# Channel mix cut into pieces of 12 matmuls and placed between attention heads, on one core

## The chip, the cores and the metric

The kernel is written in Bass, engine by engine, for one NeuronCore of one Trainium2 chip. Each engine (PE is TensorE, ACT ScalarE, DVE VectorE, POOL GpSimd, SP SyncE) runs its own instruction list strictly in the order written; semaphores are all that ties them together. The metric is the device time of one execution in microseconds (us), lower is better.

## The reference, cut to what matters

Input x is [4, 512, 512] (4 sequences of 512 tokens, 512 features). The output is the input plus two branches that both start from its layer norm xn.

```python
xn = layernorm(x)
# branch 1: RWKV style block
x1 = ln(xn); xln = ln(x1)
r = sigmoid(mix(xln, shift(xln)) @ Wr);  vmix = sum_t((xln @ Wv) * decay_t)
x2 = xn + r * (vmix @ Wo + bo)
xc = ln(ln(x2))
vc = square(relu(shift(xc) @ Wck)) @ Wcv      # channel mix, 512 -> 2048 -> 512
branch1 = x2 + sigmoid(xc @ Wcr) * vc
# branch 2: attention (16 heads of 32) and a mixture of 8 experts, top 2
q, k, v = rms(xn) @ Wq, Wk, Wv
h = softmax(causal(q k^T / sqrt(32))) v
xp = xn + h @ Wo
rows = rms(xp); route = top2(rows @ Wr)
branch2 = xp + sum_e weight_e * (silu(rows Wg_e) * (rows Wu_e)) Wd_e
out = x + branch1 + branch2
```

Precision: every large product is done as three fp32r matmuls (`mm3`, lines 49 to 51): each operand is split in a rounded high half and a remainder, and high*high, high*low, low*high are summed in one PSUM bank. The rounding copy is an ACT instruction, the remainder a subtraction on DVE or POOL.

## The kernel before

Four stages follow each other, each a `Block` whose end all engines wait for.

**Time mix** (`time_mix_phase`): norms, v, r, and rc = sigmoid(xc @ Wcr) for the four sequences; writes xn, x2, rc and the halves of xc to DRAM. The change leaves it as it is but for how its semaphores are given back.

**Attention** (`attention_phase`), one sequence b after another in a loop: q, k and v projections (`q`, `k`, `v`, 48 matmuls of 512 columns each), then `heads(b)`, then the output projection `project(b)`, the RMS norm, the transposes (`turn_rows`), the router's logits and the routing on DVE (`routing`, a chain of 15 small dependent operations). q and k are gathered by DMA into "stacks" of 96 rows (high, low, high), so that one matmul gives the exact product. `heads(b)` runs steps s = 0 to 25. Step s computes the scores of head s (`scores`, 4 matmuls plus 4 small bf16 matmuls for the causal mask), of which DVE takes the row maxima (`maxima`). The maxima are transposed in three sets (heads 0-3, 4-9, 10-15), negated, and sent by DMA into row 96 of the stack; from step LAG = 8 on, head s - 8 has its scores computed again transposed with the maximum subtracted (`turned_scores`), ACT takes the exponential in three parts and rounds it (DVE does the rounding for the last eight heads), DVE forms the remainder (`split_probs`), and head s - 10 is multiplied by its values (`head_output`, 12 matmuls). For the first eight steps of every sequence PE has scores alone.

**Channel mix** (`channel_mix_phase`): the 2048 hidden features in 8 chunks of 256; for each chunk the four sequences: `up` (24 matmuls of 512 columns into two banks), relu on ACT, square on DVE, rounding on ACT, remainder on DVE, `down` (24 matmuls into four banks), with `up` of the next sequence issued before `down` of this one. A weight chunk is split once and used for four sequences. `acc`, 128x8192 in SBUF, holds the sum for all tokens. In the same stage POOL places the routed tokens (`Router`): 32 indirect DMAs, lines 688 to 692, that scatter 128 entries each into a table in DRAM.

**Experts** (`experts_phase`): 23 tiles of 256 rows, 4 weight chunks each; writes `acc` to `out` and adds the experts' rows by indirect DMA. POOL waits for the write of `acc` (`base_out`) before its loop.

The order of work is written out by hand in each engine's function; there is no planner.

## Time and profile before

| | |
|---|---|
| time, median of 3 runs | 2159.82 us (2156.29 to 2162.97) |
| the profiled execution | 2163.49 us; its span 2161.7 us; mean granted clock 0.922 |
| PE busy | 1914.1 us, 89% |
| DVE busy | 1202.4 us, 56% |
| ACT busy | 935.3 us, 43% |
| POOL busy | 551.5 us, 26% |

The span is the time from the first to the last instruction. "Granted clock" is the share of 2.4 GHz at which TensorE was let run: 0.50 is its lower level of 1.2 GHz, 1.00 is 2.4 GHz, and a value between is a stretch with both. Matmuls are pipelined and their ends are modelled, so the duration of one matmul (0.39 us for 512 columns) is longer than the distance from one start to the next; the distance is what counts for throughput.

### The profile page before, as it was taken

The numbers are of one execution on the slowest core, as the hardware profiler recorded it, in microseconds if no ns is written. First come the engines' busy times: TensorE is split into PE (matmuls) and PEld (weight loads), VectorE is DVE, ScalarE is ACT, GpSimd is POOL, SyncE is SP. The second block draws the span as 40 slices with busy tenths as digits, with TensorE's granted clock in tenths as the row PEclk, the third lists the DMA queues.
The fourth block names the chain that finished last, engine by engine and source line by source line (L and its number), as shares of the span: only waits on it lengthen the run. The fifth ranks groups of instructions, "written<-read, shape, count | busy, mean of one in ns | idle before, by whom it ended". The sixth has DMA issues, their size and how long they took to land. (4 is left out here: it accounts for less than half of the span.)

```text
span 2161.7 us, 30419 instructions
## 1 busy us (share of the span) xinstructions
PE 1914.1 (89%) x10850; PEld 1634.4 (76%) x10850; DVE 1202.4 (56%) x1794; ACT 935.3 (43%) x1505; POOL 551.5 (26%) x536
## 2 busy tenths in 40 slices
PE   3878667898889889767999997999999999999997
PEld 2666455686677676555888886999999999999986
DVE  6887334835726736543555557555555555555543
ACT  4454333634625525422222222555555555555553
POOL 3233220010010010152000004334444353434443
PEclk9989876996996987877999998999999999999998
DMA  4332352251270260270002015756666565756562
GB/s 175 118 117 97 137 156 60 79 144 33 78 168 8 78 157 1 78 277 9 32 19 79 0 40 208 280 196 202 201 213 216 203 209 201 228 196 206 193 194 49
DMA packets 70275, 288.21 MB, mean 133 GB/s; under 512 B 10375, under 2 KB 10631, under 8 KB 51922
## 3 DMA queue, kind: packets, MB, share of 16 engines
q1 hardware_dynamic: 56514, 262.84, 35.0%
q0 software_dynamic: 11552, 20.55, 5.6%
q10 hardware_dynamic: 2160, 4.19, 0.5%
q8 instruction: 28, 0.46, 0.1%
q14 instruction: 21, 0.17, 0.0%
HBM read 220.47 MB, written 45.84 MB: 123 GB/s over the span
## 5 line engine op out<-in xcount | busy, mean ns | idle before, releaser
L49 PE MATMUL bank<-ex_x_hi,ex_w_hi 128*128 128x256 f32 x1472 | 419.0, 285 | 5.2 <-issue 5.2
L50 PE MATMUL bank<-ex_x_lo,ex_w_hi 128*128 128x256 f32 x1472 | 417.4, 284 | 0.0
L51 PE MATMUL bank<-ex_x_hi,ex_w_lo 128*128 128x256 f32 x1472 | 417.3, 284 | 0.0
L1215 DVE TENSOR_TENSOR ex_w_lo<-ex_stage,ex_w_hi 128x2048 fp32r<-128x2048 f32 x138 | 249.9, 1838 | 147.4 <-ACT ex_w_hi L1160 141.0
L49 PEld LDWEIGHTS bank<-ex_x_hi,ex_w_hi 128*128 128x128 f32 x1472 | 283.1, 192 | 8.2 <-issue 5.6
L50 PEld LDWEIGHTS bank<-ex_x_lo,ex_w_hi 128*128 128x128 f32 x1472 | 283.2, 192 | 2.7
L51 PEld LDWEIGHTS bank<-ex_x_hi,ex_w_lo 128*128 128x128 f32 x1472 | 283.1, 192 | 0.0
L1099 POOL TENSOR_TENSOR ex_a_lo<-ex_a,ex_a_hi 128x256 fp32r<-128x256 f32 x184 | 176.6, 980 | 393.5 <-ACT ex_a_hi L1180 381.5
L1175 ACT ACTIVATE ex_gate<-bank 128x256 f32<-128x256 f32 x184 | 70.7, 384 | 240.7 <-PE bank L51 240.7
L721 ACT ACTIVATE cm_relu<-bank 128x512 f32<-128x512 f32 x64 | 38.3, 599 | 256.8 <-PE bank L51 220.7
L1943 PE MATMUL bank<-at_k,at_q 96*128 96x512 f32 (+3 forms) x256 | 115.4, 546 | 38.0 <-DMA at_k<-at_ones 26.9
L49 PE MATMUL bank<-ex_w_hi,ex_a_hi 128*128 128x512 f32 x368 | 144.6, 393 | 1.7 <-POOL ex_a_lo L1099 1.7
L50 PE MATMUL bank<-ex_w_lo,ex_a_hi 128*128 128x512 f32 x368 | 144.3, 392 | 0.0
L51 PE MATMUL bank<-ex_w_hi,ex_a_lo 128*128 128x512 f32 x368 | 143.2, 389 | 0.0
L1802 DVE TENSOR_REDUCE at_row_max<-bank 128x1 f32<-128x128 f32 (+3 forms) x256 | 107.6, 483 | 44.1 <-PE bank L1945 44.1
L1160 ACT ACTIVATE ex_w_hi<-ex_stage 128x2048 fp32r<-128x2048 f32 x69 | 131.2, 1901 | 1.6 <-DMA ex_stage<-in_w_moe 1.6
L1814 DVE TENSOR_TENSOR at_p_lo<-at_p_full,at_p_hi 128x1280 fp32r<-128x1280 f32 x64 | 95.5, 1493 | 58.8 <-ACT at_p_hi L1673 57.7
L763 DVE SCALAR_TENSOR_TENSOR cm_a<-bank,cm_relu 128x512 f32<-128x512 f32 x64 | 44.2, 690 | 135.4 <-ACT cm_relu L721 122.6
L49 PE MATMUL bank<-cm_x_hi,cm_w_hi 128*128 128x512 f32 x256 | 102.8, 401 | 8.4 <-DVE cm_w_lo L756 8.4
L1667 ACT ACTIVATE at_p_full<-bank 128x512 f32<-128x512 f32 (+1 forms) x192 | 87.0, 526 | 53.0 <-PE bank L1957 51.5
L1236 DVE TENSOR_TENSOR ex_a<-ex_gate,bank 128x256 f32<-128x256 f32 x184 | 72.6, 415 | 65.0 <-ACT ex_gate L1175 61.0
L1943 PEld LDWEIGHTS bank<-at_k,at_q 96*128 96x128 f32 x256 | 75.4, 297 | 41.9 <-DMA at_k<-at_ones 22.7
(268 smaller groups left out, 4484.1 us busy)
## 6 DMA issues: line engine op xcount, KB each, us to landing
ex_stage<-in_w_moe SPq DMA_DIRECT2D x69, 1536.0 KB, 6.3
first_w<-in_w_moe SPq DMA_DIRECT2D x23, 1536.0 KB, 7.5
at_q<-at_q_hi SPq DMA_DIRECT2D x32, 256.0 KB, 5.2
at_k<-at_k_hi SPq DMA_DIRECT2D x32, 256.0 KB, 6.3
cm_stage<-in_w_cm SPq DMA_DIRECT2D x8, 1024.0 KB
tm_x_in<-in_x SPq DMA_DIRECT2D x4, 1024.0 KB, 7.2
scratch_xn<-tm_xn SPq DMA_DIRECT2D x4, 1024.0 KB, 5.3
tm_xn_res<-scratch_xn SPq DMA_DIRECT2D x4, 1024.0 KB, 9.0
```

Of the source, the lines that this page charges most:

```text
L49: pe.matmul(out, lhsT=w_hi, rhs=x_hi, start=first, stop=False)
L50: pe.matmul(out, lhsT=w_hi, rhs=x_lo, start=False, stop=False)
L51: return pe.matmul(out, lhsT=w_lo, rhs=x_hi, start=False, stop=last)
L1099: pool.tensor_tensor(a_lo[:, s % 2, m, :], a[:, m, :], a_hi[:, s % 2, m, :].bitcast(F32), ALU.subtract).then_inc(a_lo_ready, 1)
L1160: act.activation(w_hi[:, c % 2, UP], stage[c][:, UP], ACT.Copy).then_inc(wu_hi_ready, 1)
L1175: act.activation(gate[:, m, :], up_bank[m][:, 0:TILE], ACT.Silu).then_inc(gate_ready, 1)
L1215: return dve.tensor_tensor(dst, src, hi.bitcast(F32), ALU.subtract)
L1236: dve.tensor_tensor(a[:, m, :], gate[:, m, :], up_bank[m][:, TILE:2 * TILE], ALU.mult).then_inc(a_full, 1)
L1667: act.activation(p_full[i % 2][:, at:at + cols], psum[3 + n][:, 0:cols], ACT.Exp, scale=QK_SCALE).then_inc(exp_ready, 1)
L1802: dve.tensor_reduce(row_max[:, j, n:n + 1], psum[bank0 + bank][:, col:col + (j + 1) * P], AX.X, ALU.max).then_inc(max_step, 1)
L1814: dve.tensor_tensor(p_lo[i % 2][:, :], p_full[i % 2][:, :], p_hi[i % 2][:, :].bitcast(F32), ALU.subtract).then_inc(p_lo_ready, 1)
L1943: pe.matmul(out[:, col:col + (j + 1) * P], lhsT=q2[0:STACK, i, j * P:(j + 1) * P], rhs=k2[0:STACK, i, 0:(j + 1) * P], start=True, stop=False)
```

## The change

The attention stage and the channel mix stage are replaced by two others.

**`project_phase`** computes q, k and v of all four sequences in one stage, with PSUM banks 4-7 for q and the transposes and 0-3 for k and v, and writes the halves of q and k and the unsplit v to DRAM.

**`heads_phase`** runs all 64 heads as one pipeline of steps 0 to 70, unrolled on every engine (no loops). LAG is 5; the maxima are turned in sets of 4 heads. The q and k stacks are rings of 8 slots filled by six DMAs of 64 KB per head, v comes per pair of heads. Channel mix and output projection are "pieces" of 12 matmuls of 512 columns: `up` (128 hidden features of one sequence), `down` (128 tokens, four hidden chunks) and `proj`; 64 + 64 + 16 = 144 pieces, in the order up, up, up, up, down, down, down, down, with the four `proj` of a sequence let in when its heads are done. Steps 0 to 4 and 64 to 70 have two pieces each, the 59 steps between share 94, and pieces 118 to 143 follow after the last step. All `up` pieces share one PSUM bank and all sums share another. Weights come in slices of 128x512 through a ring of six, and are loaded and split again for every sequence: 144 slices. There is no `acc` for all tokens: `out` is filled with x by DMA, and x2, the projection's rows and the gated channel mix are added to it by accumulating DMAs from POOL, each of which waits for the one before. Routing of a sequence is done after its projection; the scatter of the router's table (32 indirect DMAs) stands in POOL's list at piece 129.

```diff
+    LAG = 5
+    SLOTS = 8
+    SET = 4
+    RAW = 6
+    DEEP = 4
+    CHUNKS = I_CM // (DEEP * P)
+    STEPS = N + LAG + 2
+    FIRST_PROJ = HEADS + LAG + 2
+    def pieces_before(s):
+        early = 2 * min(s, LAG)
+        middle = 94 * min(max(s - LAG, 0), N - LAG) // (N - LAG)
+        late = 2 * max(s - N, 0)
+        return early + middle + late
+        S_BANK, T_BANK = psum[0:2], psum[2:4]
+        o_bank, up_bank, sum_bank, misc_bank = psum[4:8]
...
+        @block.sync
+            load_slot(0)
+            for w in range(RAW):
+                load_slice(w)
+            load_slot(1)
+            load_mix(0)
+            for g in range(2, SLOTS):
+                load_slot(g)
+            sp.dma_start(vecs[:, :, :], d["vecs"]).then_inc(const_in, 16)
+            sp.dma_start(wr[:, :, :], d["w_r"]).then_inc(const_in, 16)
...
+        @block.gpsimd
+            def add_rows(k, b, j, src):
+                pool.wait_ge(added, 16 * adds_before[k])
+                at = b * S + j * P
+                pool.dma_start(d["out"][at:at + P, :], src[:, j, :], accum_op=ALU.add, max_dma_last_dim=4 * H).then_inc(added, 16)
...
+                if k == count_at + 2:
+                    pool.wait_ge(table_filled, 16)
+                    pool.wait_ge(route.step, route.SLOTS)
...
+        @block.scalar
+            def begin(k):
+                for w in fresh[k]:
+                    weight(w)
+                kind, b, c, m = order[k]
+                if kind == "up":
+                    n = ups_before[k]
+                    act.wait_ge(up_done, n + 1)
+                    act.activation(relu[:, m, :], up_bank[:, :], ACT.Relu).then_inc(relu_ready, 1)
+            for s in range(STEPS):
+                i = s - LAG
+                ks = pieces(s)
+                for k in late:
+                    finish(k)
+                for k in ks[:1]:
+                    begin(k)
+                if 0 <= i < N:
+                    exps(i, 0)
+                    exps(i, 1)
+                for k in ks[:1]:
+                    finish(k)
+                if 1 <= i <= N and i % 2 == 0:
+                    inverse_sums(i // 2 - 1)
+                if 0 <= i < N:
+                    exps(i, 2)
+                    high_p(i)
...
+                for k in ks[1:]:
+                    begin(k)
+                if s % SET == 0 and SET <= s <= N:
+                    max_row(s // SET - 1)
+                late = ks[1:]
...
+        @block.vector
+            def begin(k):
+                kind, b, c, m = order[k]
+                if kind == "up":
+                    n = ups_before[k]
+                    dve.wait_ge(relu_ready, n + 1)
+                    dve.scalar_tensor_tensor(a[:, m, :], up_bank[:, :], 0.0, relu[:, m, :],
+                                             ALU.max, ALU.mult).then_inc(a_full, 1)
...
+                for w in fresh[k]:
+                    weight(w)
+            def finish(k):
+                if kind == "up":
+                    dve.wait_ge(a_hi_ready, n + 1)
+                    dve.tensor_tensor(a_lo[:, m, :], a[:, m, :], a_hi[:, m, :].bitcast(F32),
+                                      ALU.subtract).then_inc(a_lo_ready, 1)
+            for s in range(STEPS):
+                if s < N:
+                    maxima(s, 0)
+                    maxima(s, 1)
+                for k in late:
+                    finish(k)
+                if 1 <= i <= N:
+                    low_p(i - 1)
+                if s % 2 == 0 and 0 <= s // 2 - 4 < N // 2:
+                    output(s // 2 - 4)
+                for k in ks[:1]:
+                    begin(k)
+                if s < N:
+                    maxima(s, 2)
...
+                for k in ks[:1]:
+                    finish(k)
...
+                for k in ks[1:]:
+                    begin(k)
+                late = ks[1:]
...
+        @block.tensor
+            def up(k, b, c, m):
+                pe.wait_ge(w_lo_ready, slice_at["up", b, c, m] + 1)
+                n = ups_before[k]
+                if n:
+                    pe.wait_ge(a_full, n)
+            def total(k, left_hi, left_lo, j):
+                n = sums_before[k]
+                if n:
+                    pe.wait_ge(sum_taken, n)
+            def down(k, b, c, j):
+                pe.wait_ge(w_lo_ready, slice_at["down", b, c, DEEP - 1] + 1)
+                pe.wait_ge(a_lo_ready, ups_before[k])
+            pe.wait_ge(x_zero, 3)
+            pe.wait_ge(consts_ready, CONSTS)
+            pe.wait_ge(const_in, 32)
+            for s in range(STEPS):
+                if s < N:
+                    scores(s, 0)
+                    scores(s, 1)
+                for k in ks[:1]:
+                    piece(k)
+                if s < N:
+                    scores(s, 2)
+                if 0 <= i < N:
+                    turned(i, 0)
+                    turned(i, 1)
+                if 1 <= i <= N:
+                    head_output(i - 1)
+                if 0 <= i < N:
+                    turned(i, 2)
+                for k in ks[1:]:
+                    piece(k)
+                if s % SET == 0 and SET <= s <= N:
+                    turn_maxima(s // SET - 1, misc_free[0])
+            for k in range(pieces_before(STEPS), PIECES):
+                piece(k)
```

```diff
 def experts_phase(...)
-            for b in range(B):
-                sp.dma_start(d["out"][b * S:(b + 1) * S, :].rearrange(tokens, p=P),
-                             acc[:, b * TT:(b + 1) * TT, :]).then_inc(base_out, 16)
...
-            pool.wait_ge(base_out, 16 * B)
 def build(nc, d):
         time_mix_phase(nc, psum, ident[:, :], d)
-        attention_phase(nc, psum, ident[:, :], ident_bf[:, :], causal[:, :], causal_t[:, :], d)
-        channel_mix_phase(nc, psum, d, routing, acc, stage, first_tile)
-        experts_phase(nc, psum, ident[:, :], routing, first_tile, acc, d)
+        project_phase(nc, psum, ident[:, :], d)
+        heads_phase(nc, psum, ident[:, :], ident_bf[:, :], causal[:, :], causal_t[:, :], routing, first_tile, route, d)
+        experts_phase(nc, psum, ident[:, :], routing, first_tile, d)
```

A piece that is the second of its step is called late below: ACT and DVE finish it only in the next step.

## Rows read from the trace of the kernel before

**Rows 1.** Busy time by stage: us, PE, PEld, DVE, ACT, POOL busy (instructions), granted clock, DMA share, GB/s
```profile
0.00:268.60 268.60, 184.70 (x744) 142.54 (x744) 186.54 (x396) 116.64 (x169) 89.23 (x82) 0.91 0.35 129
268.60:932.90 664.30, 559.47 (x2864) 440.76 (x2864) 351.77 (x587) 288.43 (x532) 55.33 (x24) 0.83 0.32 88
932.90:1333.30 400.40, 363.69 (x1538) 292.62 (x1538) 216.09 (x320) 90.27 (x136) 63.66 (x60) 0.94 0.19 69
1333.30:2161.70 828.40, 806.21 (x5704) 758.49 (x5704) 447.97 (x491) 439.98 (x668) 343.29 (x370) 0.99 0.61 202
```

**Rows 2.** Same view, two stretches of the first sequence's heads
```profile
345.00:355.00 10.00, 10.00 (x41) 6.93 (x40) 7.59 (x21) 0.59 (x1) 0.95 (x1) 0.50 0.00 1
...
375.00:385.00 10.00, 9.51 (x65) 7.65 (x65) 7.95 (x15) 7.58 (x13) 0.00 (x0) 1.00 0.00 0
```

**Rows 3.** Timeline of PE, one step between heads: start, us, instruction
```profile
377.05 0.50 PE L1943 MATMUL bank<-at_k,at_q 96*128 96x512 f32 x1 [0.49 <-DVE at_row_max L1802]
...
378.17 0.48 PE L1955 MATMUL bank<-at_q,at_k 97*128 97x512 f32 x1
...
379.28 0.47 PE L1979 MATMUL bank<-at_p_hi,at_v_hi 128*128 128x512 f32 x1
...
381.15 0.45 PE L1943 MATMUL bank<-at_k,at_q 96*128 96x512 f32 x1
```

**Rows 4.** Busy time in two stretches of the channel mix
```profile
971.00:995.00 24.00, 9.71 (x20) 4.75 (x19) 1.38 (x2) 0.60 (x1) 15.94 (x17) 0.61 0.02 2
...
1060.00:1120.00 60.00, 60.00 (x263) 49.07 (x262) 34.42 (x48) 16.11 (x23) 0.00 (x0) 1.00 0.09 35
```

**Rows 5.** Timeline of all engines inside the first of them
```profile
985.48 0.59 PE L50 MATMUL bank<-cm_w_lo,cm_a_hi 128*128 128x512 f32 x1 [1.52 <-issue]
985.79 0.96 POOL L690 DMA_INDIRECT scratch_table<-rt_pair,rt_places  x1 [0.30 <-issue]
...
989.00 0.59 PE L51 MATMUL bank<-cm_w_hi,cm_a_lo 128*128 128x512 f32 x1 [2.94 <-issue]
```

**Rows 6.** Groups of instructions: busy us, mean ns | idle before, releaser
```profile
L1814 DVE TENSOR_TENSOR at_p_lo<-at_p_full,at_p_hi 128x1280 fp32r<-128x1280 f32 x64 | 95.5, 1493 | 58.8 <-ACT at_p_hi L1673 57.7
L775 DVE TENSOR_TENSOR acc<-bank,acc 128x512 f32<-128x512 f32 x128 | 85.4, 686 | 29.8 <-PE bank L51 24.7 <-issue 2.9 <-remote 2.2
L763 DVE SCALAR_TENSOR_TENSOR cm_a<-bank,cm_relu 128x512 f32<-128x512 f32 x64 | 44.2, 690 | 135.4 <-ACT cm_relu L721 122.6 <-issue 12.6
L1673 ACT ACTIVATE at_p_hi<-at_p_full 128x1280 fp32r<-128x1280 f32 x32 | 40.7, 1272 | 17.6 <-PE bank L1981 17.4
L721 ACT ACTIVATE cm_relu<-bank 128x512 f32<-128x512 f32 x64 | 38.3, 599 | 256.8 <-PE bank L51 220.7 <-issue 20.9 <-remote 15.2
```

**Rows 7.** Timeline, the step's maxima and exponentials, four and three together
```profile
379.37 1.68 DVE L1802 TENSOR_REDUCE at_row_max<-bank 128x1 f32<-128x128 f32 x4
379.50 1.36 ACT L1667 ACTIVATE at_p_full<-bank 128x512 f32<-128x512 f32 x3 [0.29 <-PE bank L1957]
```

**Rows 8.** Timeline, start of the attention stage
```profile
268.67 0.38 SPq L1513 DMA_DIRECT2D at_xn<-scratch_xn  x1
...
270.59 1.04 SPq L1563 DMA_DIRECT2D at_w_stage<-in_w_at  x2
...
288.12 0.76 PE L49 MATMUL bank<-at_x_hi,at_w_hi 128*128 128x512 f32 x1 [3.18 <-DVE at_x_lo L1774]
```

**Rows 9.** Timeline of DVE, first and last of 12 routing operations
```profile
927.41 0.19 DVE L1858 TENSOR_REDUCE at_top<-at_logits 128x4 f32<-128x32 f32 x1
...
929.87 0.16 DVE L1871 TENSOR_TENSOR at_gap<-at_top 128x4 f32<-128x4 f32 x1
```

**Rows 10.** DMA issues: KB each, us from issue to landing
```profile
scratch_xn<-tm_xn SPq DMA_DIRECT2D x4, 1024.0 KB, 5.3
scratch_rc<-tm_mix ACTq DMA_DIRECT2D x4, 256.0 KB, 2.0
```

**Rows 11.** Timeline, PE in the experts' first tile
```profile
1363.61 0.50 PE L49 MATMUL bank<-ex_w_hi,ex_a_hi 128*128 128x512 f32 x1 [0.83 <-POOL ex_a_lo L1099]
```

More of the change, by code:

```diff
@@ new lines, in high_x, with high @@
+            def high_x(b):
+                for c in range(HC):
+                    act.wait_ge(x_turned, b * HC + c + 1)
+                    act.activation(x_hi[:, b % 2, c, :], psum[HC + c][:, :], ACT.Copy,
+                                   scale=vecs[:, V_W1, c:c + 1]).then_inc(x_hi_ready, 1)
+            def high(dst, bank, done, ready, out, b):
+                for m in range(HC):
+                    act.wait_ge(done, b * HC + m + 1)
+                    if b and m == 0:
+                        act.wait_ge(out, b * 16)
+                    act.activation(dst[:, m, :], psum[bank + m][:, :], ACT.Copy).then_inc(ready, 1)
@@ L1817, in output @@
-            def output(b, n):
-                c, half, _, _ = stack(2 * n)
-                own = slice(half * PAIR, (half + 1) * PAIR)
-                dve.wait_ge(rec_ready, b * HEADS + 2 * n + 2)
-                dve.tensor_tensor(o[own, c, :], psum[6 + n % 2][0:PAIR, :], sums_rec[0:PAIR, :],
-                                  ALU.mult).then_inc(o_ready, 1)
-            def heads(b, more):
-                for s in range(HEADS + LAG + 3):
-                    if s < HEADS:
-                        maxima(b, s, 3 * (s % 2) if s < LAG else 0)
-                    if s == LAG - 2 and more:
-                        mean(0, b + 1)
-                    if s >= LAG + 4 and (s - LAG) % 2 == 0:
-                        output(b, (s - LAG - 4) // 2)
-                    if LAG <= s < HEADS + LAG:
-                        split_probs(b, s - LAG)
-                    if s == WO_AT:
-                        low_wo(b)
@@ L1908, in _, with low_x, low @@
-            low_o(B - 1)
-            residual(B - 1)
-            routing(B - 1)
+            def low_x(b):
+                for c in range(HC):
+                    dve.wait_ge(x_hi_ready, b * HC + c + 1)
+                    dve.scalar_tensor_tensor(x_lo[:, b % 2, c, :], psum[HC + c][:, :], vecs[:, V_W1, c:c + 1],
+                                             x_hi[:, b % 2, c, :].bitcast(F32), ALU.mult,
+                                             ALU.subtract).then_inc(x_lo_ready, 1)
+            def low(dst, hi, bank, hi_ready, ready, out, b):
+                for m in range(HC):
+                    dve.wait_ge(hi_ready, b * HC + m + 1)
+                    if b and m == 0:
+                        dve.wait_ge(out, b * 16)
+                    dve.tensor_tensor(dst[:, m, :], psum[bank + m][:, :], hi[:, m, :].bitcast(F32),
+                                      ALU.subtract).then_inc(ready, 1)
@@ L1912, in _, with turn @@
+            mean(0)
+            low_w(0)
+            dve.wait_ge(vecs_in, 16)
+            low_x(0)
+            low_w(1)
+            low_w(2)
+            for b in range(B):
+                low(q_lo, q_hi, HC, q_hi_ready, q_lo_ready, q_lo_out, b)
+                if b + 1 < B:
+                    mean(b + 1)
+                low(k_lo, k_hi, 0, k_hi_ready, k_lo_ready, k_lo_out, b)
+                if b + 1 < B:
+                    low_x(b + 1)
         @block.tensor
         def _(pe):
-            def turn(src, bank, done):
+            def turn(b):
+                pe.wait_ge(norm_ready, b * TT + TT)
@@ L1922, in by_feature @@
+            def by_feature(n, b, bank, done):
                 for m in range(HC):
+                    if n == 1 and b:
+                        pe.wait_ge(v_ready, (b - 1) * TT + m + 1)
                     for k in range(HC):
@@ L1949, in turned_scores @@
-            def turned_scores(n):
-                i = stack(n)[3]
-                for kt in range(TT):
-                    bank, col = PT_AT[kt]
-                    out = psum[3 + bank]
-                    pe.matmul(out[:, col:col + (TT - kt) * P], lhsT=k2[0:STACK + 1, i, kt * P:(kt + 1) * P],
-                              rhs=q2[0:STACK + 1, i, kt * P:S], start=True, stop=False)
-                    last = pe.matmul(out[:, col:col + P], lhsT=ident_bf, rhs=causal_t, start=False, stop=True)
-                last.then_inc(turned_scores_done, 1)
```

1626 lines of the change are left out of this document (837 added, 789 removed).

## The prediction

> **What bounds the kernel now.** I read the busy time by stage first [rows 1]. Time mix (268.6 us) and experts (828.4 us) are hardly touched. The change lives in the attention stage, 664.3 us, and the channel mix, 400.4 us: together 1064.7 us. In the experts PE is busy 97% at clock 0.99. In attention the clock is 0.83 and PE idles 105 us, although no other engine is above 53%. The stretches show why: while a sequence has only scores to compute, the clock is 0.50, and 41 matmuls fill 10 us; once heads flow, it is 1.00 with 65 matmuls in 10 us [rows 2]. In the channel mix nearly all loss is in one place: from 971 to 995 PE gets 20 matmuls in 24 us, at its lower clock in most of it, with "issue" as what it waited for, while POOL issues one indirect DMA after another [rows 4, 5].
>
> So PE sets the end of both stages, and what can be won is its idle time and slow clock. Its necessary work at full clock:
> - A head: scores 377.05 to 378.17 (1.12 us), transposed scores to 379.28 (1.11), values to 381.15 (1.87): 4.10 us [rows 3]. 64 heads: 262.
> - A piece: 263 matmuls in 60 us are 0.228 us each [rows 4]. I take 0.23, so 12 matmuls are 2.76 us; 144 pieces: 397.
> - q, k, v: 4 x 144 x 0.23 = 132.
>
> **Part 1, the projection stage.** The first projection matmul stood 19.5 us after the first load of its stage [rows 8]; the order up to there is the same: 19.5. Then 132 of matmuls, 7.5 for the cold start and three sets of transposes, and the drain: evacuation 0.6, a 1 MB store 5.3 [rows 10], issue and barriers 5: 11. q and k use different banks and the norm of the next sequence (about 9 us of ACT, DVE and POOL) lies beside k's 11 us, so I cost these at nothing. If that cover fails, 2 us per sequence. Sum 170: from 268.6 + 2 (semaphores given back) to 441.
>
> **Part 2, the head stage before its first matmul.** PE waits for `const_in`, and `vecs` and `wr` stand behind 6 + 6 + 6 + 2 + 36 = 56 DMAs in SP's list. SP issues a DMA in 0.52 us (two in 1.04) [rows 8]: 58 x 0.52 = 30, landing 4. PE starts at 441 + 34 = 475. Bounds: 25 if small DMAs issue faster, 45 if the 6.6 MB ahead of them hold the queue.
>
> **Part 3, PE's work in it.** 262 + 397, rows turned and logits 18, maxima 6, 5 for the cold start: 688.
>
> **Part 4, PE's new waits.** The order is fixed on every engine, so I walked the steps. A step with one piece is 4.1 + 2.8 = 6.9 us of PE, one with two 9.6. Per step DVE has maxima 1.68 [rows 7], remainder 1.49, and for `up` 0.69 + 0.69 [rows 6], half an output 0.34, a weight slice 0.6 (an estimate from the 0.69 of other operations on 512 columns) and 0.5 of values: about 6.0. ACT has 1.36 [rows 7] + 1.27 + 0.60 for relu [rows 6], and by the same row 0.6 for each of rounding and weight slice, 1.1 for sums and values: 5.5. Both fit, with DVE the closer. What does not fit is latency:
> - Step 0 to 4, nothing between the pieces but scores: 8.
> - `up` after a late `up` (12 times by the placement): the bank is free after relu 0.60 and product 0.69 plus 0.1, but PE has only two parts of scores, 0.75, to fill: 0.65 each, and DVE's remainder of the probabilities then comes 0.5 later than wanted: 14.
> - `down` after a late `up` (7 times): it needs the last remainder. DVE does product to 1.35, weight to 2.0, the next head's first three maxima to 3.4, then the remainder to 4.1; PE wants it at 0.75: 3.35 each, 23. This is the dearest wait in the pipeline.
> - Maxima row: ACT copies it after everything else of a step; copy 0.6, DMA 2.0 [rows 10]. In the 6 single steps of the 16 it lands 1.3 late: 8.
> - Output bank shared by all pairs: in some 12 odd single steps the inverse of the sums is 0.5 late: 6.
> - Routing of three sequences: 12 chained operations from 927.41 to 930.03 [rows 9], 2.6 on DVE, of which some 2 show: 6.
> - Steps 64 to 70: 6.
> - The 26 pieces after the last step: nothing is between them. Four `up` cost 3 x 1.35 and the change to `down` 2.65, four `down` 3 x 0.7 = 8.8 per eight pieces: 26, and 10 for the last routing, placing and norm.
> - The 32 scatters: 32 x 1.26 = 40 us, each 0.96 and 0.30 before it [rows 5]. Before, PE got 20 matmuls in 24 us of such a train, worth 4.6 at full rate: 19.4 lost [rows 4]. The new code is as new to the engines at that place: 20. Bounds 0 and 40.
> - After the last piece: one accumulating DMA, table, first tile's rows: 12. No row shows an accumulating direct DMA; a plain 1 MB store lands in 5.3, a 256 KB one in 2.0 [rows 10]; I take 6 for the last, bounds 2 and 20.
> Sum 139. Below it could be 60 if an engine ahead covers half of these, above 220 if DVE's wait on ACT lengthens each step.
>
> One rule of the Trainium skill speaks against the burst's term. "Runtime: NRT & Kernel Launch", section "Instruction fetch mechanics", says that a long straight program is streamed by each engine's sequencer itself and the crossing of a block is mostly hidden, while a taken branch can cost a fetch stall. That speaks for unrolled code. The trace agrees in that no such "issue" stretch stands in the long straight lists of the heads, and disagrees in the 24 us of rows 4 and 5. By the rule the 20 would be 0 and the time 2107.
>
> **Part 5, experts.** No write of `acc`. POOL had waited for it, but PE lost only 0.83 us [rows 11]: -1, so 827.
>
> **Sum.** 475 + 688 + 139 = 1302, where the experts began at 1333.3 [rows 1]. 1302 + 827 = 2129 span, and 1.8 around it (2163.49 less 2161.7): 2131, which is 32.5 less than the profiled run. That run was 3.7 above the median, so I say 2127 against 2159.82, 1.5% faster. What the old stages wasted, eight steps of scores at half clock in each sequence, does go; start-up, unfilled latencies and the tail take most of it back: 170 + 34 + 688 + 139 + 2 = 1033 against 1064.7.
>
> **Rivals.**
> - Engine coupling (slower). DVE is at 6.0 of 6.9 us in a single step with `up`; if each wait adds to the next, DVE becomes the bound of the step. Its place is DVE's list between `low_p` and the last maxima. 1 us per step over 64 steps gives 2191; it decides for slower from 0.5 us per step. For it: DVE's remainder already waited 57.7 us on ACT in 32 heads [rows 6]. Against: with a piece, PE's own step is 2.8 us longer than it was then.
> - Supply of the unrolled lists (slower). If the 36 accumulating DMAs from POOL starve the engines as the scatters did, at 1.5 us each: 54 more, 2181. Against: they are single, not a train.
> - Waits mostly hidden. Pieces give every latency 2.76 us of cover; late `up` to `down` and the tail stay, half the rest goes, and the burst with it: 139 becomes 75, 2063.
> - The burst costs nothing, with the rest as forecast: 2107.
> - The clock does not stay up: the change doesn't do what it says. The tail has PE at 2.76 of 4.1 us. A stretch with PE busy 9.5 of 10 us was at 1.00 [rows 2], one with 9.7 of 24 at 0.61 [rows 4]; the tail lies between. If the last 26 pieces ran at half clock, 70 more: 2197.
>
> **How the numbers follow.** A measurement of this kernel can tell 0.3% from no change, 6.5 us: 2153.3 to 2166.3. Forecast 0.34 (its own range 2095 to 2155), burst free 0.12, waits hidden 0.22, coupling 0.18, supply 0.08, clock 0.06. Faster: 0.34 + 0.12 + 0.22 less 0.05 at the forecast's upper end: 0.63. Same: that 0.05 and 0.04 from the lower ends of the slow cases: 0.09. Slower: 0.32 less 0.04: 0.28. The range reaches into both sides: 2045 to 2195.
>
> **What would show it.** Project stage near 170 us with PE without gaps over 2 us. First matmul of the head stage 34 us after its first load. Clock 1.00 from there to the tail. Waits of `down` for the remainder `a_lo`, some 3.4 us each, 7 times, and of `up` for `a`. A stretch of "issue" waits on all engines while POOL scatters, some 20 us. Steps of 6.9 and 9.6 us; if they are 8 and 11, coupling is right and I am wrong. If PE's idle sum in the head stage after its start is under 80, the third rival is right.

## The result, and the profile after

The changed kernel takes 2183.52 us (median of 8 runs, 2169.88 to 2185.85) against 2159.01 (8 runs, 2155.81 to 2165.19): ratio 1.0099, 95% interval [1.0075, 1.0123]. It is 1.0% slower; 2127 had been forecast. The profiled execution took 2173.18 us with a span of 2171.3.

Busy time by stage: time mix, projections, the head stage before its first matmul, the rest of it, experts (columns as in [rows 1]):

```profile
0.00:269.40 269.40, 184.52 (x744) 142.57 (x744) 186.55 (x396) 116.68 (x169) 89.26 (x82) 0.91 0.35 129
269.40:440.20 170.80, 145.79 (x640) 118.29 (x640) 43.26 (x58) 65.57 (x117) 8.39 (x11) 0.91 0.47 170
440.20:464.60 24.40, 0.00 (x0) 0.00 (x0) 2.83 (x6) 2.62 (x5) 0.00 (x0) 0.50 0.89 255
464.60:1344.00 879.40, 736.61 (x3778) 575.36 (x3778) 492.20 (x917) 430.74 (x800) 82.85 (x97) 0.95 0.43 115
1344.00:2171.30 827.30, 805.53 (x5704) 758.04 (x5704) 447.93 (x491) 440.01 (x668) 344.32 (x370) 0.99 0.61 197
```

Projections (forecast 170) and experts (827) came out as worked out. The start was 10 us better than forecast: a small DMA takes SP 0.42 us, where [rows 8] had 0.52:

```profile
448.40 0.42 SPq L1002 DMA_DIRECT2D hd_q<-scratch_q_hi  x1
```

All of the error is in the fourth row: 879 for 827. The same view, cut at steps 0 to 4, 5 to 63, 64 to 70, the 26 pieces after the last step (the tail), and what follows the last matmul:

```profile
464.60:515.70 51.10, 41.90 (x170) 31.53 (x170) 23.78 (x46) 13.02 (x24) 4.47 (x4) 0.87 0.99 267
515.70:1117.90 602.20, 547.45 (x2963) 431.60 (x2962) 376.19 (x699) 347.12 (x642) 29.71 (x32) 0.97 0.42 113
1117.90:1190.30 72.40, 60.26 (x285) 46.75 (x284) 39.88 (x57) 36.68 (x65) 3.48 (x4) 0.95 0.45 128
1190.30:1326.80 136.50, 87.00 (x362) 65.48 (x362) 50.96 (x114) 33.92 (x71) 41.31 (x53) 0.91 0.25 62
1326.80:1344.60 17.80, 0.00 (x0) 0.01 (x1) 1.39 (x2) 0.01 (x1) 3.91 (x5) 0.63 0.47 101
```

By the forecast's own terms these were 46, 578, 60, 132 and 12. The clock of the second row is 0.97, although no other engine is near its limit: something makes PE fall back to 1.2 GHz now and then. The timeline shows where. PE and DVE around one change from `up` to `down` (start, us, instruction, idle before it and what ended it):

```profile
625.15 0.23 PE L1506 MATMUL bank<-causal_t,ident_bf 128*128 128x128 bf16 x1
627.53 0.49 DVE L1395 TENSOR_TENSOR hd_v_lo<-hd_v_raw,hd_v_hi 128x128 fp32r<-128x128 f32 x2 [2.93 <-ACT hd_v_hi L1234]
627.94 0.69 DVE L1348 TENSOR_TENSOR hd_a_lo<-hd_a,hd_a_hi 128x512 fp32r<-128x512 f32 x1
628.73 0.76 PE L48 MATMUL bank<-hd_down_hi,hd_a_hi 128*128 128x512 f32 x1 [3.35 <-issue]
629.29 0.63 PE L49 MATMUL bank<-hd_down_lo,hd_a_hi 128*128 128x512 f32 x1
...
631.42 0.57 PE L48 MATMUL bank<-hd_down_hi,hd_a_hi 128*128 128x512 f32 x1
631.83 0.39 PE L49 MATMUL bank<-hd_down_lo,hd_a_hi 128*128 128x512 f32 x1
```

PE pauses 3.35 us, and the next six matmuls start 0.43 us apart; from the eighth on it is 0.23. So this pause cost 3.35 and 1.4 more (3.10 us for seven matmuls that take 1.7 elsewhere). The release is put down to "issue", but the remainder `a_lo` ended at 628.63, just before. It stood behind `low_v`, which waited 2.93 us for ACT, ahead of it in DVE's list.

The length of a pause alone does not say whether the half clock follows. The same `down`, the first of step 64, stood 3.16 us in this execution and in one of the unaltered kernel in a later session (`e_same_2` below):

```profile
1121.12 0.77 PE L48 MATMUL bank<-hd_down_hi,hd_a_hi 128*128 128x512 f32 x1 [3.16 <-DVE hd_down_lo L1303]
1121.69 0.63 PE L49 MATMUL bank<-hd_down_lo,hd_a_hi 128*128 128x512 f32 x1
```
```profile
1121.11 0.47 PE L48 MATMUL bank<-hd_down_hi,hd_a_hi 128*128 128x512 f32 x1 [3.16 <-DVE hd_down_lo L1303]
1121.42 0.39 PE L49 MATMUL bank<-hd_down_lo,hd_a_hi 128*128 128x512 f32 x1
```

The first took 5.26 us for its twelve matmuls, the second 2.87. In the first execution a pause of 1.97 us (at 752.0) was followed by a piece of 5.26, one of 2.51 (at 940.7) by one of 2.87.

A `down` piece without any pause, and the `up` behind it:

```profile
1139.44 0.48 PE L48 MATMUL bank<-hd_down_hi,hd_a_hi 128*128 128x512 f32 x1
1142.32 0.40 PE L48 MATMUL bank<-hd_x_hi,hd_up_hi 128*128 128x512 f32 x1
```

2.88 us for twelve matmuls, where I had taken 2.76 from the average of [rows 4]: the first after scores takes 0.32, the others 0.233.

PE's waits in the head stage: us in total, times, longest:

```profile
PE bank L48 <- DVE hd_a L1310: 46.4, 23, 15.6
PE bank L1490 <- DMA hd_wr<-in_w_r: 34.0, 1, 34.0
PE bank L48 <- issue: 25.0, 11, 3.4
PE bank L48 <- DVE hd_down_lo L1303: 18.4, 7, 3.2
```

The scatters, as in [rows 5], inside the tail:

```profile
1282.00 0.63 ACT L1159 ACTIVATE hd_down_hi<-hd_raw 128x512 fp32r<-128x512 f32 x1 [19.27 <-remote]
...
1288.69 0.96 POOL L1132 DMA_INDIRECT scratch_table<-rt_pair,rt_places  x1 [0.30 <-issue]
1293.18 0.60 ACT L1168 ACTIVATE hd_relu<-bank 128x512 f32<-128x512 f32 x1 [10.55 <-remote]
...
1294.65 0.77 PE L48 MATMUL bank<-hd_x_hi,hd_up_hi 128*128 128x512 f32 x1 [15.65 <-DVE hd_a L1310]
```

PE had written the bank that the relu reads by 1279.0, and ACT was free from 1282.6; it stood 10.55 us, until 3.5 us after the last scatter had been made, and PE waited 15.65 for it. (Of the 19.27 before, all but 6 was a wait for PE's sums.) At the end POOL's accumulating DMAs wait for each other:

```profile
1330.96 0.86 POOL L1105 DMA_DIRECT2D out<-hd_acc  x1 [7.88 <-DMA out<-hd_acc]
1335.35 0.86 POOL L1105 DMA_DIRECT2D out<-hd_acc  x1 [3.54 <-DMA out<-hd_acc]
```

### The profile page after: what moved, and what is told of

Its sections match the earlier page's. It is cut to its first block and busy times, and to the rows that moved or that the text cites. A ratio compares the mean times of both kernels' runs of the same rounds, so it can differ in the third digit from the quotient of the medians.

```text
span 2171.3 us, 30573 instructions
## 1 busy us (share of the span) xinstructions
PE 1872.4 (86%) x10866; PEld 1594.3 (73%) x10866; DVE 1172.8 (54%) x1866; ACT 1055.6 (49%) x1758; POOL 524.8 (24%) x560
## 5 line engine op out<-in xcount | busy, mean ns | idle before, releaser
L1214 ACT ACTIVATE hd_p_full<-bank 128x512 f32<-128x512 f32 (+1 forms) x192 | 94.4, 528 | 140.7 <-PE bank L1506 139.9
L48 PE MATMUL bank<-hd_down_hi,hd_a_hi 128*128 128x512 f32 x256 | 112.1, 438 | 47.7 <-issue 22.8
L48 PE MATMUL bank<-hd_x_hi,hd_up_hi 128*128 128x512 f32 x256 | 108.1, 422 | 46.4 <-DVE hd_a L1310 46.4
L1366 DVE TENSOR_REDUCE hd_row_max<-bank 128x1 f32<-128x512 f32 (+3 forms) x256 | 113.0, 483 | 36.4 <-PE bank L1492 36.3
L1105 POOL DMA_DIRECT2D out<-hd_acc x16 | 14.0, 875 | 437.4 <-DVE hd_acc L1327 401.2
L1490 PE MATMUL bank<-hd_k,hd_q 96*128 96x512 f32 (+3 forms) x256 | 81.4, 375 | 37.0 <-DMA hd_wr<-in_w_r 34.0
L50 PE MATMUL bank<-hd_down_hi,hd_a_lo 128*128 128x512 f32 x256 | 106.6, 416 | 0.0
L49 PE MATMUL bank<-hd_down_lo,hd_a_hi 128*128 128x512 f32 x256 | 106.1, 415 | 0.0
```

Of the source, the lines that this page charges most:

```text
L48: pe.matmul(out, lhsT=w_hi, rhs=x_hi, start=first, stop=False)
L49: pe.matmul(out, lhsT=w_hi, rhs=x_lo, start=False, stop=False)
L50: return pe.matmul(out, lhsT=w_lo, rhs=x_hi, start=False, stop=last)
L1214: act.activation(p_full[:, i % 2, at:at + T_COLS[part]], T_BANK[n % 2][:, 0:T_COLS[part]], ACT.Exp, scale=QK_SCALE).then_inc(exp_ready, 1)
L1366: i = dve.tensor_reduce(row_max[:, j, g % (2 * SET):g % (2 * SET) + 1], S_BANK[n % 2][:, col:col + (j + 1) * P], AX.X, ALU.max)
L1490: pe.matmul(bank[:, col:col + (j + 1) * P], lhsT=q2[0:STACK, g % SLOTS, j * P:(j + 1) * P], rhs=k2[0:STACK, g % SLOTS, 0:(j + 1) * P], sta ...
```

## The experiments

Ratios are to the kernel before in the same session. In the stretches, "tail" is the 26 last pieces, "end" the time from their last matmul to the first instruction of the experts' stage; they are 136.5 and 17.8 us in the profile above.

**The changed kernel again** (two sessions, no edit).

> The changed kernel once more, as the base of the other runs. Its eight runs fell into two groups, 2170 to 2173 us at a mean granted clock of 0.950 and 2181 to 2186 at 0.944 to 0.947. Expected 2183 again, ratio 1.010. If a profile of the longer kind is caught, the 11 us should stand in one stage with a lower granted clock there; if they are spread over all stages the two groups are not a matter of one stretch.

> The changed kernel unaltered, on the same chip as its neighbours here, because the chips differ (the kernel before took 2158 us in one session and 2141 in another). Expected ratio 1.010; and if the difference of the chips stands in the scatter train, the tail of 26 pieces differs with it.

Ratios 1.0099 [1.0064, 1.0134] and 1.0112 [1.0094, 1.0130]. Both profiles are of the longer kind. Steps 5 to 63 took 605.4 and 602.6 us (602.2 above), the tail 146.4 and 150.9:

```profile
1189.30:1340.20 150.90, 97.30 (x363) 72.98 (x362) 50.93 (x114) 34.10 (x71) 40.92 (x53) 0.84 0.23 56
```

So the longer kind is longer mostly in the tail, at clock 0.84 for 0.91. The profile first shown is of the shorter kind, 10 us under the median. The difference is for the larger part half clock and not waiting: by the count used in the table further down, the tail loses 4.4 us to the half clock in the first profile, 11.8 and 14.9 in these two, while PE's pauses in it sum to 49.5, 52.0 and 53.6. Before the tail's first piece PE stood 2.6 us in all three; the piece took 3.05, 4.43 and 5.48.

**DVE: the late remainder ahead of the maxima.**

```diff
+                for k in late:
+                    finish(k)
                 if s < N:
                     maxima(s, 0)
                     maxima(s, 1)
-                for k in late:
-                    finish(k)
```

> Only the order in VectorE's list changes: the remainder of a late `up` piece now stands ahead of the next head's first two groups of maxima. Theory (the wait of `down` for that remainder costs twice, as a gap and as a lower clock after it): the seven gaps of 3.2 to 3.4 us between a late `up` and a `down` shrink to about 1.3 (relu 0.60, product 0.69, rounding 0.63, remainder 0.69, less 0.9 of PE's scores), 14 us; the pieces after them, which took 4.1 to 5.3 us instead of 2.87, are back at 2.87, another 10 us. Together -24: about 2159, ratio 0.999. Rival 1 (the clock falls for another reason, the mean load): 14 us only, the long pieces stay: ratio 1.0035. Rival 2 (coupling of the engines): the maxima come 0.7 us later, the next scores wait for their bank, and nothing is won: ratio 1.010.

1.0092 [1.0061, 1.0123]: 24 us expected, 3 found, which the intervals can't tell from none. The trace (second and third line: start of a `down`):

```profile
627.00 0.49 DVE L1395 TENSOR_TENSOR hd_v_lo<-hd_v_raw,hd_v_hi 128x128 fp32r<-128x128 f32 x2 [2.92 <-ACT hd_v_hi L1234]
861.71 0.77 PE L48 MATMUL bank<-hd_down_hi,hd_a_hi 128*128 128x512 f32 x1 [2.33 <-DVE hd_down_lo L1303]
862.27 0.63 PE L49 MATMUL bank<-hd_down_lo,hd_a_hi 128*128 128x512 f32 x1
```

I had the cause of these gaps half right. Where `up` was a late piece and maxima stood in the way, 3.4 us became 2.3 (the rest is relu, product, a weight slice and the remainder, one after another), and the half clock after it stayed: 4.4 us for the piece. One gap fell from 2.31 to 1.17 and was followed by a piece of 2.87 (4.42 before); another fell to 1.27, and its piece still took 4.67. In two of the cases (here 3.35, unchanged) `up` was the step's first piece, and its remainder stood behind `low_v`, which the forecast had not looked at. After step 63 there are no maxima and 3.15 stayed.

**PE: a `down` waits for each chunk when it comes to it.**

```diff
-                pe.wait_ge(w_lo_ready, slice_at["down", b, c, DEEP - 1] + 1)
-                pe.wait_ge(a_lo_ready, ups_before[k])
-                total(k, lambda q: a_hi[:, q, :], lambda q: a_lo[:, q, :], j)
+                def ready(q):      # called before the three matmuls of chunk q, j == 0 only
+                    pe.wait_ge(w_lo_ready, slice_at["down", b, c, q] + 1)
+                    pe.wait_ge(a_lo_ready, ups_before[k] - DEEP + 1 + q)
+                total(k, lambda q: a_hi[:, q, :], lambda q: a_lo[:, q, :], j, ready)
...
```

The first `proj` of a sequence waits for its weight slices in the same way.

> The first of four `down` pieces waits for each activation chunk and weight slice when it comes to it, not for all four before its first matmul, so nine of its twelve matmuls can run ahead of the last remainder. Theory: each `up` to `down` gap of 3.35 in the heads and 2.85 after them falls by 2.07 us (nine matmuls of 0.23), 11 times, and the half-clock pieces behind them go: 23 + 12 = 35 us: ratio 0.994. The wait then shows inside the piece, 1.3 us. Rival (the clock answers to any pause, not to its length): the long pieces stay and 20 us are won: ratio 1.001. Rival (the remainder is only the last of several things late): under 10 us.

0.9894 [0.9858, 0.9930]: 44 us off the changed kernel, and faster than the one before. Steps 5 to 63:

```profile
511.90:1088.20 576.30, 535.37 (x2963) 421.50 (x2964) 375.75 (x699) 347.35 (x642) 29.65 (x32) 1.00 0.45 120
```

26 us less, for the same instructions: PE idle 40.9 us for 54.8 (the length of the row less PE's busy time), time lost to half clock in the pieces 1.6 for 11.6, clock 1.00 for 0.97.

**PE: useless work in the pause.**

```diff
+                if j == 0:
+                    ...
+                    for _ in range(9):
+                        pe.matmul(sum_bank[:, :], lhsT=a_hi[:, 0, 0:P], rhs=down_hi[:, 0, :], start=True, stop=True)
                 pe.wait_ge(w_lo_ready, slice_at["down", b, c, DEEP - 1] + 1)
                 pe.wait_ge(a_lo_ready, ups_before[k])
```

> Nothing is moved: before the first `down` of each chunk PE runs nine extra matmuls of 512 columns (2.07 us) on operands that are ready, into the bank that the piece then overwrites, and only then waits for the last remainder as before. So a pause of 3.35 us becomes 2.07 of useless work and 1.3 of pause. Theory (the lower clock in the piece after such a gap comes from PE's pause): the long pieces of 4.1 to 5.3 us go back to 2.87, 10 to 15 us less in the head stage although no wait is shorter, offset by up to 2 us at the few places where there was no wait to fill: ratio 1.010 less 0.005 = 1.005. Rival (the clock has another cause than the pause, or dummy work adds its own time): long pieces stay, ratio 1.010 or above.

1.0052 [1.0030, 1.0074], with 1.0112 [1.0094, 1.0130] for the unaltered kernel in the same session: as the theory had it. The place shown above, now:

```profile
623.16 2.34 PE L1567 MATMUL bank<-hd_down_hi,hd_a_hi 128*128 128x512 f32 x9
626.70 0.47 PE L48 MATMUL bank<-hd_down_hi,hd_a_hi 128*128 128x512 f32 x1 [1.20 <-issue]
627.00 0.39 PE L49 MATMUL bank<-hd_down_lo,hd_a_hi 128*128 128x512 f32 x1
```

No operand was ready sooner, 144 matmuls came on top, and the kernel is 12 us (0.6%) faster: after 1.20 us of pause the matmuls take 0.39, after 3.35 they took 0.63. This shows that PE's standing idle brings the half clock. Whether the one long pause or the idle time of the stretch as a whole decides, it doesn't separate.

**The scatters: left out, and spread.** `e_no_scatter` makes only the first of the 32 and its experts work on the table's fill, so only its head stage is to be read. `e_paced` and `e_paced_2` are one kernel in two sessions:

```diff
                 if k == count_at + 2:
                     ...
-                    ...                                  # all 32
+                if k >= count_at + 2:
+                    first = k - count_at - 2
+                    if kind == "up":
+                        pool.wait_ge(a_full, ups_before[k])
+                    else:
+                        pool.wait_ge(sum_taken, sums_before[k])
+                    for i in range(32 * first // (PIECES - count_at - 3), ...):
```

> 31 of the 32 scatters that write the routing table are left out, so the experts work on the fill of the table; only the head stage is to be read. Theory (the train of indirect DMAs keeps the other engines' instruction lists from being supplied): the gap of 15.65 us at 1294 falls to the 1.5 us of every other `up` after `up`, and the two pieces at half clock (4.65 and 5.47 us) become 3.0, in all 14 + 4 = 18 us in the stretch from the first tail piece to the last, 136.5 to about 119. Rival (the engines' own lists wait for something else at that place, such as a code page that has to be fetched anyway): the 15 us gap stays, at most 3 us less.

> The 32 scatters are all there, but spread over the last 15 pieces, two or three in each, each group held until PE has come to its piece. Leaving them out had taken 17 us (against the shorter kind of run) to 27 us (against the longer) from the tail. Theory A (an uninterrupted train starves the others' instruction lists, and any pause lets them through): the tail is near 120 us as without them, ratio 1.001. Theory B (each scatter costs the others a fixed share, wherever it stands): no change, the gaps are cut smaller but their sum stays 17 or more: ratio 1.009.

> The spread scatters once more, now beside the unaltered kernel on one chip. Before, its tail took 119.9 us, as long as with the scatters left out, but its ratio to the kernel before was 1.0119. Theory A (a pause between groups lets the other engines' lists through): tail 120, and 10 to 17 us less in all than the unaltered kernel beside it. Theory B (the train costs the same however it is cut): within 4 us of it.

Left out: 1.0012 [0.9994, 1.0029], with 1.0099 for the unaltered kernel in the same session. Spread: 1.0119 [1.0102, 1.0136] in a session where the kernel before took 2141.59, and 1.0019 [1.0004, 1.0033] in the session of the unaltered kernel's 1.0112. The tail with them left out:

```profile
1193.40:1313.30 119.90, 84.60 (x362) 63.88 (x362) 50.96 (x114) 33.93 (x71) 10.62 (x22) 0.97 0.28 70
```

And with them spread (second session; 119.9 us in the first):

```profile
1197.30:1322.80 125.50, 90.17 (x362) 67.93 (x362) 51.00 (x114) 33.98 (x71) 39.55 (x50) 0.92 0.27 61
```

By the medians of one session each, leaving the train out took 18 us off (2163.01 for 2181.37) and spreading it 22 (2161.40 for 2183.33). The two tails of the shorter kind, 136.5 and 119.9, differ by 17. Against the tails of the longer kind it would be 27 to 31, but part of that is the half clock behind pauses that have nothing to do with scatters: the spread tail just shown has 5.5 us more of it than the one without scatters, at pauses of 35.4 and 35.3 us. In groups of two or three the train costs nearly nothing (theory A): the pauses fell from 53.6 in the unaltered kernel of that session.

The other session, of `e_paced`, `e_ends`, `e_ring` and `e_all`, is no test of that, for there an unbroken train held nobody up either. `e_ends` below leaves the train as it was: 32 scatters, 1.26 us apart, from 1231.7 to 1272.8. Its tail, and ACT inside the train:

```profile
1170.70:1296.50 125.80, 90.45 (x362) 68.05 (x362) 50.94 (x115) 33.93 (x71) 42.83 (x55) 0.92 0.28 68
```
```profile
1260.16 0.63 ACT L1163 ACTIVATE hd_down_hi<-hd_raw 128x512 fp32r<-128x512 f32 x1 [13.58 <-PE bank L50]
1262.89 0.60 ACT L1172 ACTIVATE hd_relu<-bank 128x512 f32<-128x512 f32 x1 [2.10 <-PE bank L50]
```

Both waits end with PE's sums and none with "remote", and PE's pauses in the tail sum to 35.3 us, as without scatters. `e_ring`, with its train unbroken too, has none either. So the spread kernel had nothing to win in that session, and its 1.0119 fits that. The kernel before was 17 us faster there, about what its own train cost in [rows 4]; no profile of it was taken in that session, so that this is the reason is not shown. What changes between sessions stays open; the session of `e_same` and this one have the same chip number on record.

> The kernel before once more, for its profile on this chip: where the scatters stood between 971 and 995 us it had 20 matmuls in 24 us. If the chips differ in what the train costs, this stretch is shorter on a chip where the whole kernel takes 2141 and the same where it takes 2158.

It took 2155.74 us, beside a median of 2157.55: not the fast session that was wanted, but its stretch of scatters differs from that of [rows 4]. This run:

```profile
970.00:995.00 25.00, 15.46 (x51) 10.10 (x50) 4.47 (x7) 2.03 (x4) 16.24 (x17) 0.74 0.02 1
```

The profile before:

```profile
970.00:995.00 25.00, 10.58 (x24) 5.31 (x22) 1.38 (x2) 0.60 (x1) 16.63 (x18) 0.63 0.02 2
```

27 matmuls more, and a span 7.7 us shorter. What a train costs changes from one execution to the next in the old kernel too.

**The ends.** SP's order: first head, constants, four weight slices, input, then the rest. In POOL the gathers of the experts' first tile stand before the last accumulating DMA, and (with DVE's wait for them altered to fit):

```diff
             def add_rows(k, b, j, src):
-                pool.wait_ge(added, 16 * adds_before[k])
+                if j == 0:
+                    pool.wait_ge(added, 16 * adds_before[k])
```

> Only the two ends of the head stage change. Start: the two constant loads stand second in SyncE's list and the first weight slices and the sequence's input before the other seven heads' loads, where the changed kernel has 54 DMAs ahead of the constants and PE begins 24.4 us after the stage before. Theory: PE begins its scores some 20 us sooner, waits once for the 2 MB of input, and is 12 us ahead after step 4. End: the four accumulating DMAs of a sequence no longer wait for each other and the first tile's gathers stand before the last one, where 17.85 us lie between the last matmul and the experts: 8 to 10 us. Together -20: ratio 1.001. Rival (the loads' bytes, not their order, set the start; the last adds are limited by their own landing): -5, ratio 1.008.

1.0009 [0.9992, 1.0025]. PE's first matmul, and its first of a piece:

```profile
440.21 0.76 PE L1494 MATMUL bank<-hd_k,hd_q 96*128 96x512 f32 x1 [10.27 <-DMA hd_wr<-in_w_r]
...
450.22 0.76 PE L48 MATMUL bank<-hd_x_hi,hd_up_hi 128*128 128x512 f32 x1 [8.21 <-DMA hd_x_lo<-scratch_xc_lo]
```

24 us sooner at the first, 17 at step 5 (498.8 for 515.7), the rest going to a wait for 2 MB of input; end 11.7 for 17.8. As expected, a little more at the start and less at the end. The medians agree: 2141.63 is 25 us under the spread kernel of the same session.

**Three banks in turn in the tail.**

```diff
+        def bank_of(k):
+            if k < TAIL:
+                return up_bank if order[k][0] == "up" else sum_bank
+            return psum[5 + k % 3]
...
```

> In the 26 pieces after the last head, the pieces take three PSUM banks in turn (the banks of `up`, of the sums, and the one that turned maxima), and a piece waits for the piece three before it to be read. Theory (each of these pieces waits for one bank to be read): the gaps of 1.50 after an `up` (8 of them) and of 0.88 after a sum (12) go, 12 + 11 = 23 us; of the 6.6 us gap at the routing chain 5 goes too; the 2.85 before a `down` and the scatter train stay: -25, ratio 0.998. Rival (VectorE and ScalarE are the bound once PE runs ahead): the gaps only change their place, under 8 us won.

1.0019 [1.0004, 1.0033]. The tail is 34 us shorter than in the profile above:

```profile
1187.10:1289.70 102.60, 84.46 (x363) 67.94 (x362) 50.90 (x114) 33.56 (x71) 41.68 (x52) 0.90 0.31 72
```

But 17 us of that are what the train cost in that profile, and where `e_ring` was run it cost nothing. Against the spread kernel's tail there, 119.9, the three banks are worth 17 where 25 had been expected. The end grew from 17.8 to 22.0: POOL's scatters ended at 1285, so its four accumulating DMAs came after them.

**Everything together, and three ends to it.** `e_all`: all the above, and a first `up`'s remainder ahead of `low_v`. `e_best`: scatters one train again, the last accumulating DMA ahead of the gathers, the first expert's weights asked for before the table. `e_all_2`: that with the scatters spread.

> All edits together: waits per chunk before the first `down` (measured alone -43), the remainder of a late `up` first in VectorE's step and that of a first `up` ahead of the values' remainder, the ends, the three banks, the spread scatters. If they act in different places their gains add: 43 + 3 + 20 + 25 + 15, less some 8 that the waits per chunk and the banks both count: 2183 - 98 = 2085, ratio 0.966. If what is left is bound by VectorE's and ScalarE's lists (coupling), the sum is missed by more than a third: over 2115.

> As the kernel with all edits, with three changes at its end. There the tail of 26 pieces took 91 us where 136 to 151 stood before, but 23 us lay between the last matmul and the experts, because POOL's 32 scatters (47 us with what stands between them) now end 6 us after the last piece, the gathers stood ahead of the last accumulating DMA, and that one was issued 11 us before the experts began. Now the scatters are one train again, the last accumulating DMA stands ahead of the gathers, and the first expert's weights are asked for before the table. Theory (POOL's chain of scatters, table, gathers is what the end waits for): 23 becomes 15 to 17, ratio 0.9758 less 0.003 = 0.973, if the train does not starve the other engines. Rival (the train without pauses starves them again, as it did in the changed kernel): the tail is 10 to 20 us longer, ratio 0.98.

> The last kernel with its scatters spread over the pieces again, nothing else. Theory (a train without pauses keeps ScalarE's list from being supplied: it waited 14.3 us until the train had ended, and the tail took 117.6 us against 91.1): the tail is back near 91 to 95 us, and the end stays near the 17.5 us it now has or falls to 15: 26 - 23 + 6 = about 25 us less than the last kernel where the train hit it, ratio 0.9763 - 0.011 = 0.965. Rival (the two kernels differ by chance, the train hits one execution and not another): within 8 us of it, ratio 0.973 or above, with a `remote` wait of 8 us or more on ScalarE or VectorE in the tail.

Ratios 0.9758 [0.9742, 0.9774], 0.9763 [0.9747, 0.9779], 0.9678 [0.9662, 0.9695]. The tail of `e_all`:

```profile
1139.90:1231.00 91.10, 83.16 (x363) 65.47 (x362) 50.84 (x114) 33.57 (x71) 39.55 (x50) 0.94 0.36 82
```

That of `e_best`, and ACT in it:

```profile
1141.80:1259.40 117.60, 91.50 (x363) 70.29 (x362) 50.88 (x114) 33.35 (x71) 42.32 (x54) 0.85 0.28 66
```
```profile
1240.16 0.60 ACT L1177 ACTIVATE hd_relu<-bank 128x512 f32<-128x512 f32 x1 [14.33 <-remote]
```

PE itself, inside one `up` piece, whose twelve matmuls have no wait between them:

```profile
1231.02 0.39 PE L49 MATMUL bank<-hd_x_lo,hd_up_hi 128*128 128x512 f32 x1 [2.20 <-issue]
...
1233.12 0.59 PE L50 MATMUL bank<-hd_x_hi,hd_up_lo 128*128 128x512 f32 x1 [1.71 <-issue]
```

And that of `e_all_2`:

```profile
1141.80:1242.40 100.60, 89.63 (x362) 69.80 (x362) 51.08 (x114) 33.22 (x71) 39.33 (x51) 0.88 0.32 76
```

In time the gains add: `e_all` took 2088.90 where 2085 was expected (not in the ratio, 0.966, as the kernel before was faster there too; the 15 us counted for the spread scatters were to be had without spreading in that session). Its end was 22.9 us, because PE now finishes before POOL's 32 scatters. `e_best` shortened the end to 17.5, but its train held ACT for 14.33 us and lost 26 in the tail: the rival came true. With the scatters spread the tail is at 100.6, with 4.3 us of such a wait left and an end of 18.6, and the kernel at 2090.52 against 2160.95, 3.2% faster than the kernel before. It falls between the theory's 91 to 95 and the rival. `e_best` and `e_all_2` come from two sessions with one profile each, in both of which the kernel before took its usual time (2158.82 and 2160.95).

## Why the prediction was wrong

Counted over the 880 us from the first matmul to the experts (a piece lasts from its first matmul to the next instruction, less the pause; time over 2.87 in pieces beyond 3.2 is put down to the half clock):

| term | forecast | measured |
|---|---|---|
| 144 pieces at full clock | 397 | 413 (2.87 each) |
| half clock (forecast: the cold start) | 5 | 23 |
| heads, rows, logits, maxima | 286 | 299 |
| pauses, end included | 139 | 141 |
| drain before a pause | 0 | 4 |

- **New waits: right in sum, by luck in part.** 139 forecast, 141 found. The waits of `up` for the product, of `down` for the remainder (seven at 3.2 to 3.4 us, forecast 3.35), of the sums' bank in the tail and the tail's sum of 56 (measured 49) are where they were said to be. But two of the 3.35 had another cause (`low_v`), and no step of mine held DVE's wait for ACT inside its own list.
- **The failed step: a pause was priced by its length alone.** I counted the late `up` to `down` at 7 x 3.35 and wrote "Clock 1.00 from there to the tail". Behind most of these PE ran at 1.2 GHz for some seven matmuls and more: 12 us in steps 5 to 63, 23 in all in this execution and 30 and 33 in the two of the longer kind, against 5. The useless matmuls show that PE's idling is the cause, and the waits per chunk that it need not be: half clock in steps 5 to 63 fell to 1.6. What decides whether a given pause is followed by it is open: the same 3.16 us was and was not, and pauses of 1.3 us were in two places. The rows for it were there: [rows 5] has matmuls of 0.59 us, at a clock of 0.61 in [rows 4], behind pauses of 1.52 and 2.94, and I read them as the scatters' doing alone.
- **A piece mis-sized.** 2.87, not 2.76: 16 us. 263 matmuls in 60 us [rows 4] is 0.228, a long run without a change of kind; I even rounded up, but left out the first matmul after scores, 0.32.
- **Heads and rows** are 13 over: the heads' matmuls took 271 for 262, in part at half clock, rows and logits 21 for 18, the maxima 6 as forecast.
- **Burst.** Forecast 20, found 17 by the profiles and 18 to 22 by the medians: right where the train costs anything, and nothing in one session of the six, which was the rival at 2107. The 10 us between that profile and the median are for the larger part half clock, not the burst. The Trainium skill ("Runtime: NRT & Kernel Launch", "Instruction fetch mechanics") says that the next instructions are streamed while the engine works and a crossing is mostly hidden. With single DMAs about, and under the train in `e_ends` and `e_ring`, the runs agree; under the train in the other sessions they do not (ACT stood 10.55 us). That PE waits for no semaphore there is shown where it stopped for 2.20 and 1.71 us inside a piece; that instructions are what is missing, for PE and behind ACT's "remote", is my reading.
- **Start and end.** 24 for 34, 18 for 12: the chain of four accumulating DMAs, each waiting for the one before, not one.
- **Rivals.** Engine coupling would have had steps of 8 and 11. Counted from one head's first scores to the next, waits included, the median step took 7.5 us with one piece and 11.0 with two, so by that sign alone it would nearly stand. But it works by adding waits, and the waits came out as forecast (141 for 139); what is over in a step is the piece's size and the half clock. The time it gave (2191) is near, its mechanism is not. (By my own band of 0.3% it decides for slower from 0.6 us per step, not 0.5.) Supply by 54 more and waits mostly hidden (139 becoming 75) are ruled out by the same 141. The clock rival named the tail alone; the loss was at the longer pauses, in the heads as well. In the first profile the tail's gaps of 0.9 to 1.5 left pieces at 3.02; in `e_same_2` one of 1.32 was followed by a piece of 4.40.

The profiled run adds up: 42 us over the forecast's span = 53 in the table, 10 less at the start, 1 in rounding. The median adds 10 for the longer kind and 4 because the profile before stood above its median.

So the expected gain of 32 us was to be had only if the fixed order left no such pause. The old stages lost their time in eight steps of scores at half clock; the new one loses it in many small places, some of them paid twice. Of the 53 us in the table the half clock is 18, the piece's size 16 and the heads and rows 13: no single term made the error.

## What to carry to other kernels

Price a pause of PE as its length plus what the clock may take after it (here nothing to 2.6 us a pause, and not the same in every execution), and let a consumer wait per chunk instead of for a whole set: one edit of that kind moved this kernel by 2%. Before a ratio of two sessions is compared, look whether the kernel they are measured against changed too. When a fixed order is written, list for each wait all that stands ahead of its producer in that producer's own list, with what those items wait for. Put pauses into a train of indirect DMAs, and once PE is fast, check whether the train itself has become the chain that ends last.

## What the runs showed of the hardware

- After a pause of 3.35 us six matmuls started 0.43 us apart before the pitch was 0.23 again. The length of the pause does not decide it: after 3.16 us at one place the twelve matmuls took 5.26, 2.86 and 2.87 in three executions, after 1.97 us 5.26, after 2.51 us 2.87, after 1.27 us 4.67 in `e_late_first`.
- PE at work on a result that nobody reads keeps the clock: 16 times nine such matmuls made the kernel 0.6% faster.
- Under 32 indirect DMAs from POOL, 1.26 us apart, ACT stood 10.6 us (14.3 in another kernel) and went on 3.5 to 4 us after the last. With waits between groups PE's pauses in the tail were 18 us shorter in one session (35.4 for 53.6), the kernel 22. In another session the same unbroken train held up no engine (`e_ends`, `e_ring`).
